# Layer 2's closing: Silu on ScalarE in place of tanh and a product on VectorE

## The chip, the cores and the metric

The kernel runs on one core of one Trainium2 chip. The metric is the device time of one execution in microseconds (us); lower is better. The engines are named as in the profile: PE is TensorE, ACT is ScalarE, DVE is VectorE, POOL is GpSimd.

## The reference, cut to what matters

Four layers follow each other. Each takes x, normalises it, computes a sequence mixer s and a feed-forward result g, and adds their gated product:

```python
xn = _layernorm(x, axis=-1)
s = _L2_attn_ref(xn, ...)                 # windowed attention plus a gated attention on 64 latents, then @ w_out
g = _silu(_L2_ffn_ref(xn, theta, phi, theta_noise, phi_noise))
x = x + s * g

def _L2_ffn_ref(x, theta, phi, theta_noise, phi_noise):
    real = jnp.einsum('bti,io->bto', x, jnp.cos(theta + theta_noise))
    imag = jnp.einsum('bti,io->bto', x, jnp.sin(phi + phi_noise))
    return jnp.sqrt(real * real + imag * imag)
```

x has 8 sequences of 512 tokens with 128 features. The function silu(m) is m / (1 + exp(-m)), which is the same as m (tanh(m/2) + 1) / 2. In layer 2 its argument m is the magnitude, the square root above.

## The kernel before

The whole of x stays in SBUF. Layers 0 to 2 go through it in four chunks of two sequences each (index b is the sequence in its chunk, index c the chunk). Layer 3 then works head by head and takes over half of the time.

Layer 2 is a software pipeline written out by hand. A generator for each engine (`l2_pe`, `l2_dve`, `l2_act`, `l2_pool_engine`) runs over the same slots s = -39 to 37. Each slot holds one unit of windowed and latent attention in several stages: `UNITS2` is 32, eight units in a chunk, each of 128 tokens of one sequence. Work that is done once for a chunk is hung on a slot by `due(d)`, which gives the chunks c with 8c + d = s. So the order of instructions on each engine is fixed by the program, and only semaphores tie the engines to each other. The slots below are counted as in the code; a slot of ACT issues `exponential(s)`, and the same slot of PE ends with `turn_p(s, 0)`, the transposes that need it.

The closing of a chunk goes through these steps:

- `magnitude` (PE) multiplies with the cos and sin matrices; `square` (ACT) squares; `add` (POOL) adds the two squares into the tile moe; `root` (ACT, slot 8c + 3) takes the square root of moe in place.
- `close_tanh(c, b)` (ACT, both at slot 8c + 6) writes tanh(moe / 2) into the tile normed. The one for b = 0 is the first instruction of ACT's slot, ahead of `latent_exponential(s - 1)`. The one for b = 1 stands behind `latent_out(s - 2)` and ahead of `open_copy`, `latent_copy(s - 1)` and `exponential(s)`.
- `close_gate(c, b)` (DVE, slots 8c + 10 and 8c + 11) makes (normed + 1) moe in place. It counts `l2_gated`, on which `close` waits, and on which POOL's `add` of the next chunk waits before it writes moe again.
- `output` (PE, slot 8c + 11) multiplies with w_out; `close` (DVE, slot 8c + 13) multiplies the bank by 0.5 and by normed, and adds the result to x.

The functions that ACT computes in layer 2 are Exp, Tanh, Identity, Square and, once in a chunk, Sqrt. Layer 1 uses Silu, Tanh, Identity and Exp; its first part ends before layer 2's first closing. Layer 3 begins with a Sqrt. Where ACT needs other function tables than those that are active, the compiler puts in an instruction ACT_TABLE_LOAD; the kernel's text does not have it, and the profile books it at the line of the ACTIVATE behind it.

Order of ACT in a slot, the part that matters:

```python
for c in due(6):
    close_tanh(c, 0)
if 0 <= s - 1 < k.UNITS2:
    latent_exponential(s - 1)
...
if 0 <= s - 2 < k.UNITS2:
    latent_out(s - 2)
for c in due(6):
    close_tanh(c, 1)
for c in due(-10):
    open_copy(c, 0)
if 0 <= s - 1 < k.UNITS2:
    latent_copy(s - 1)
...
if 0 <= s < k.UNITS2:
    exponential(s)
```

Of the kernel before, what the change touches and what calls it, by code (L numbers as in the profile page):

```python
# [11 lines left out]
ACT = mybir.ActivationFunctionType  # L12
# [3 lines left out]
D = 128  # L16
# [5 lines left out]
TPB = S // P  # L22
# [23 lines left out]
class Kernel:  # L46
# [1793 lines left out]
    def layer2_prepare(self):  # L1840
        k, io, V, G = self, self.io, self.V, self.G
        W = 32
        k.l2_mom, k.l2_rstd, k.l2_norm, k.l2_pool = (
            Count(k.nc, n) for n in ("l2_mom", "l2_rstd", "l2_norm", "l2_pool"))
        k.l2w_qx, k.l2w_sc, k.l2w_sub, k.l2w_exp = (
            Count(k.nc, n) for n in ("l2w_qx", "l2w_sc", "l2w_sub", "l2w_exp"))
        k.l2w_pTA, k.l2w_pTB, k.l2w_ptA, k.l2w_ptB = (
            Count(k.nc, n) for n in ("l2w_pTA", "l2w_pTB", "l2w_ptA", "l2w_ptB"))
        k.l2w_av, k.l2w_o, k.l2w_oT, k.l2w_go, k.l2g_exp = (
            Count(k.nc, n) for n in ("l2w_av", "l2w_o", "l2w_oT", "l2w_go", "l2g_exp"))  # L1850
        k.l2_add, k.l2_root, k.l2_tanh, k.l2_gated = (
            Count(k.nc, n) for n in ("l2_add", "l2_root", "l2_tanh", "l2_gated"))
        k.l2_filled, k.l2_emptied = k.l1_filled, k.l1_emptied
        k.l2_turn = {}

        flat = k.scratch.rearrange("p i b s -> p (i b s)")
        k.qT2, k.gr2, k.gl2, k.gq2, k.rem2 = ([flat[:, 2048 * i + 1024 * j:2048 * i + 1024 * (j + 1)]
                                               .rearrange("p (b s) -> p b s", b=B) for j in range(2)]
                                              for i in range(5))
        k.oT2 = [flat[:, 10240:11264].rearrange("p (b s) -> p b s", b=B),  # L1860
                 k.hT.rearrange("p (b s) -> p b s", b=B)]
        k.nT2, k.kT2, k.v2_row, k.v2, k.gk2, k.gv2_row, k.gv2 = [], [], [], [], [], [], []
        for j in range(2):
            get = k.part if j else k.own2
            k.nT2.append(get(D, B, W + S + W))
            k.kT2.append(get(D, B, W + S))
            row = get(P, B * 2 * TPB * 288 + 64)
            k.v2_row.append(row)
            k.v2.append(row[:, 0:B * 2 * TPB * 288].rearrange("p (b j w h c) -> p b j w h c", b=B, w=2, h=16, c=9))
            k.gk2.append(get(64, B, 8, 64))  # L1870
            row = get(P, B * 72 + P)
            k.gv2_row.append(row)
            k.gv2.append(row[:, 0:B * 72].rearrange("p (b a h c) -> p b a h c", b=B, a=4, h=2))

        k.pool2 = k.shaped(k.rw_now.rearrange("p i d -> p (i d)")[:, 0:B * 128], (B, 2, 64))
        small = k.rw_before.rearrange("p i d -> p (i d)")
        k.lanes2 = []
        for b in range(B):
            k.lanes2.append(dict(
                mx=small[:, 152 * b:152 * b + 16], gmx=small[:, 152 * b + 16:152 * b + 24],  # L1880
                r=k.shaped(small[:, 152 * b + 24:152 * b + 88], (16, 4)),
                go=k.shaped(small[:, 152 * b + 88:152 * b + 152], (8, 8)),
                qx=k.part(D, 4, 4, W), p=k.part(P, 8, P), pt=k.part(P, 8, P), ox=k.part(P, 4, P),
                sq=k.part(P, 2, 2, D),
                gp=k.sT[:, b * S:(b + 1) * S].rearrange("p (h n) -> p h n", n=64),
                gpt=k.aT[:, b * S:(b + 1) * S].rearrange("p (a n) -> p a n", n=P)))
        k.l2_fills = Count(k.nc, "l2_fills")
# [262 lines left out]
    def l2_dve(self):  # L2150
        k, V, W = self, self.V, 32
# [27 lines left out]
        def divide(w):  # L2179
            c, b, i, t = k.l2_unit(w)  # L2180
            av = k.bank(4, 2).rearrange("p a (n x) -> p (a n) x", x=64)[:, :, 0:36].rearrange("p n (h c) -> p n h c", c=9)
            V.wait_ge(k.l2w_av.sem, w + 1)
            k.step(V.reciprocal(t["r"][:, :, :], av[:, :, :, 8]))
            k.step(V.tensor_tensor(t["r"][:, :, :], t["r"][:, :, :], k.same_head[:, :].unsqueeze(1)
                                   .broadcast_to([P, 16, 4]), ALU.mult))
            k.after(V, k.l2w_oT, w - 1)
            V.tensor_tensor(t["ox"].rearrange("p j (g h d) -> p (j g) h d", h=4, d=8), av[:, :, :, 0:8],
                            t["r"][:, :, :].unsqueeze(3).broadcast_to([P, 16, 4, 8]),
                            ALU.mult).then_inc(*k.l2w_o.up())
# [11 lines left out]
        def latent_largest(w):  # L2201
            c, b, i, t = k.l2_unit(w)
            k.l2_filled_by(V, b, "latent_scores", w)
            k.step(V.tensor_reduce(t["gmx"][:, :], k.bank(6 + b).rearrange("p (h n) -> p h n", n=64), AX.X, ALU.max))

        def latent_subtract(w):
            c, b, i, t = k.l2_unit(w)
            if w < 2:
                k.after(V, k.gated, 2 * CHUNKS)
            V.tensor_tensor(t["gp"], k.bank(6 + b).rearrange("p (h n) -> p h n", n=64),  # L2210
                            t["gmx"][:, :].unsqueeze(2).broadcast_to([P, 8, 64]),
                            ALU.subtract).then_inc(*k.l2_emptied[b].up())
# [52 lines left out]
            k.l2_emptied_of(V, b, "gate_remote", c, b)  # L2265
            k.stt(gr, gr, 1.0, k.bank(6 + b), ALU.add, ALU.mult).then_inc(*k.l2_emptied[b].up())

        def close_gate(c, b):
            tiles = slice(b * TPB, (b + 1) * TPB)
            t = k.normed[:, tiles, :]  # L2270
            V.wait_ge(k.l2_tanh.sem, 2 * c + b + 1)
            k.stt(t, t, 1.0, k.moe[:, tiles, :], ALU.add, ALU.mult).then_inc(*k.l2_gated.up())

        def close(c, b):
            t = k.normed[:, b * TPB:(b + 1) * TPB, :]
            x = k.xs[:, c * NT + b * TPB:c * NT + (b + 1) * TPB, :]
            V.wait_ge(k.l2_gated.sem, 2 * c + b + 1)
            k.l2_filled_by(V, b, "output", c, b)
            k.step(k.stt(t, k.bank(6 + b).rearrange("p (t d) -> p t d", d=D), 0.5, t, ALU.mult, ALU.mult))
            V.tensor_tensor(x, x, t, ALU.add).then_inc(*k.l2_emptied[b].up())  # L2280

        for s, due in k.l2_slots():
            if 0 <= s - 3 < k.UNITS2:
                divide(s - 3)
            if 0 <= s - 2 < k.UNITS2:
                latent_largest(s - 2)
            if 0 <= s - 3 < k.UNITS2:
                gate_o(s - 3)
            if 0 <= s - 2 < k.UNITS2:
                latent_subtract(s - 2)  # L2290
            for c in due(12):
                mix(c, 0)
                mix(c, 1)
            for c in due(13):
                close(c, 0)
                close(c, 1)
            if 0 <= s + 1 < k.UNITS2:
                queries_spread(s + 1)
            for c in due(10):
                close_gate(c, 0)  # L2300
            for c in due(-14):
                open_scale(c, 1)
            for c in due(-21):
                open_moments(c, 1)
            for c in due(-3):
                pool(c, 0)
            for c in due(-2):
                latents(c, 0)
                latents(c, 1)
            if 0 <= s - 1 < k.UNITS2:  # L2310
                largest(s - 1)
            for c in due(11):
                close_gate(c, 1)
            for c in due(-3):
                pool(c, 1)
            if 0 <= s - 1 < k.UNITS2:
                subtract(s - 1)
            for c in due(-15):
                open_scale(c, 0)
            for c in due(-22):  # L2320
                open_moments(c, 0)
            if 0 <= s - 3 < k.UNITS2:
                latent_divide(s - 3)
            yield

    def l2_act(self):
        k, A, W = self, self.A, 32
# [80 lines left out]
            A.wait_ge(k.l2_add.sem, 4 * c + 4)  # L2408
            A.activation(k.moe[:, :, :], k.moe[:, :, :], ACT.Sqrt).then_inc(*k.l2_root.up())

        def close_tanh(c, b):
            tiles = slice(b * TPB, (b + 1) * TPB)
            A.wait_ge(k.l2_root.sem, c + 1)
            if c:
                k.l2_emptied_of(A, b, "output", c - 1, b)
            else:
                k.after(A, k.l1_closed, 2 * CHUNKS)
            A.activation(k.normed[:, tiles, :], k.moe[:, tiles, :], ACT.Tanh, scale=0.5).then_inc(*k.l2_tanh.up())

        for s, due in k.l2_slots():  # L2420
            for c in due(-6):
# [2 lines left out]
            for c in due(-4):  # L2424
                values(c, 1, 0)
            for c in due(6):
                close_tanh(c, 0)
            if 0 <= s - 1 < k.UNITS2:
                latent_exponential(s - 1)
            for c in due(3):  # L2430
# [6 lines left out]
            if 0 <= s - 2 < k.UNITS2:  # L2437
                latent_out(s - 2)
            for c in due(6):
                close_tanh(c, 1)  # L2440
            for c in due(-10):
                open_copy(c, 0)
            if 0 <= s - 1 < k.UNITS2:
# [1136 lines left out]
```

## Time and profile before

| what | value |
| --- | --- |
| median of 3 runs | 3213.32 us (3204.18 to 3224.15) |
| the profiled execution | 3207.89 us, its span 3205.2 us |
| granted clock of PE, mean | 0.976 |
| PE busy | 3074.6 us, 96% of the span |
| DVE busy | 2382.3 us, 74% |
| ACT busy | 1830.3 us, 57%, 4246 instructions |
| POOL busy | 856.6 us, 27% |

The span runs from the first to the last instruction; 2.7 us lie around it. Layer 2's units run from about 1060 to 1500 us of the span. Busy time is what an engine spent in its instructions; waits count as idle. The granted clock is PE's clock as a share of its full speed.

### The profile page before, as it was taken

The page shows a single profiled execution, that of the slowest core. Times are in us where ns is not written, and L with a number is a line of the kernel's source. Part 1 is how long each engine was busy: PE and PEld are TensorE (multiplying, and loading weights), DVE is VectorE, ACT ScalarE, POOL GpSimd, SP SyncE. Part 2 cuts the span into 40 slices and gives each one's busy share as a digit, 9 for nine tenths or more (in the row PEclk, how much of TensorE's full clock was granted, in tenths as well). Part 3 has the DMA queues.
Part 4 walks back from the last instruction along what each step waited for, and adds up shares of the span by engine and source line. Part 5 has one row for each costly group of instructions (what it writes and reads, how often), then busy time and mean ns, then how long its engine had stood idle before and what let it go on. Part 6 is the DMA issues. An engine that isn't in the chain of part 4 may idle for free. (4 is left out here: it accounts for less than half of the span.)

```text
span 3205.2 us, 57936 instructions
## 1 busy us (share of the span) xinstructions
PE 3074.6 (96%) x20342; PEld 2414.1 (75%) x20342; DVE 2382.3 (74%) x5012; ACT 1830.3 (57%) x4246; POOL 856.6 (27%) x707
## 2 busy tenths in 40 slices
PE   5999998999999999997899999999999999999998
PEld 4777775566665677775778888888888888888887
DVE  4777876556556555556867888888888888888888
ACT  2445554545655444442756666666666666666666
POOL 2101101101101100001523444444344443444443
PEclk9999998999999899998999999999999999999999
DMA  2000101000000000002001000111000111000000
GB/s 55 2 4 28 53 27 50 1 1 1 1 1 1 1 1 1 1 1 68 14 1 23 20 12 15 22 22 23 12 20 14 23 22 23 9 22 15 23 1 27
DMA packets 43555, 53.08 MB, mean 17 GB/s; under 512 B 8646, under 2 KB 27273, under 8 KB 43273
## 3 DMA queue, kind: packets, MB, share of 16 engines
q1 hardware_dynamic: 39298, 47.02, 5.9%
q8 instruction: 168, 2.75, 0.4%
q10 hardware_dynamic: 3974, 2.37, 0.3%
q14 instruction: 115, 0.93, 0.1%
HBM read 38.63 MB, written 10.75 MB: 15 GB/s over the span
## 5 line engine op out<-in xcount | busy, mean ns | idle before, releaser
L75 PE MATMUL banks<-scratch 128*128 128x128 f32 (+3 forms) x3648 | 715.5, 325 | 11.5 <-ACT scratch L2974 8.9
L75 PEld LDWEIGHTS banks<-scratch 128*128 128x128 f32 x3648 | 482.8, 192 | 77.0 <-issue 60.0
L75 PE MATMUL banks<-lower 128*128 128x128 f32 (+2 forms) x2688 | 508.8, 355 | 4.3 <-DVE lower L1453 3.7
L75 PEld LDWEIGHTS banks<-lower 128*128 128x128 f32 (+1 forms) x2688 | 343.7, 193 | 170.4 <-issue 169.4
L75 PEld LDWEIGHTS banks<-scratch,tb 128*128 128x128 f32 x2560 | 356.6, 191 | 101.9 <-issue 61.5
L75 PE MATMUL banks<-scratch,tb 128*128 128x128 f32 x2560 | 368.5, 275 | 0.0
L3417 POOL TENSOR_TENSOR scratch<-scratch,aT 128x1024 f32<-128x1024 f32 x128 | 358.8, 2803 | 4.5 <-DVE aT L3239 4.5
L83 DVE SCALAR_TENSOR_TENSOR scratch<-scratch,tb 128x512 f32<-128x512 f32 (+3 forms) x512 | 340.0, 705 | 8.4
L3409 POOL TENSOR_TENSOR scratch<-backwards,nn 128x512 f32<-128x512 f32 x128 | 133.3, 1042 | 736.1 <-ACT nn L3329 736.1
L83 DVE SCALAR_TENSOR_TENSOR scratch<-tb,nn,banks 128x512 f32<-128x512 f32 (+3 forms) x512 | 267.8, 544 | 75.6 <-PE banks L75 71.5
L3239 DVE TENSOR_TENSOR aT<-banks,turn 64x1024 f32<-64x1024 f32 x256 | 312.9, 1222 | 5.7
L3352 ACT ACTIVATE scratch<-banks 128x384 f32<-128x384 f32 (+1 forms) x384 | 200.0, 521 | 183.0 <-PE banks L79 183.0
L75 PE MATMUL banks<-nT,w 128*128 128x512 f32 x544 | 283.0, 604 | 2.6 <-PEq L69 1.4
L3343 ACT ACTIVATE scratch<-scratch,mn 128x512 f32<-128x512 f32 (+3 forms) x512 | 282.7, 566 | 0.4 <-DVE mn L3273 0.2
L3229 DVE TENSOR_TENSOR scratch<-banks,turn 128x512 f32<-128x512 f32 x256 | 176.5, 689 | 138.3 <-PE banks L75 137.1
L3273 DVE CUSTOM_DVE_ANT_0 scratch<-scratch,tb,coef 128x512 f32<-128x512 f32 (+3 forms) x512 | 261.8, 549 | 0.0
L75 PEld LDWEIGHTS banks<-minus_half,sT 128*128 128x128 f32 x2048 | 239.6, 192 | 2.0 <-ACT sT L3322 2.0
L75 PE MATMUL banks<-minus_half,sT 128*128 128x1 f32 x2048 | 236.8, 245 | 1.2 <-ACT sT L3318 1.2
L1453 DVE TENSOR_TENSOR lower<-lower,banks 128x512 f32<-128x512 f32 x160 | 108.7, 685 | 161.1 <-ACT lower L1662 161.1
L79 PEld LDWEIGHTS banks<-ident,scratch 128*128 128x128 f32 x1408 | 171.0, 141 | 72.4 <-issue 69.6
L79 PE MATMUL banks<-ident,scratch 128*128 128x128 f32 x1408 | 219.2, 273 | 2.4 <-ACT scratch L3343 1.4
L3335 ACT ACTIVATE scratch<-scratch 128x384 f32<-128x384 f32 (+1 forms) x384 | 215.3, 561 | 8.1 <-DVE scratch L83 6.4
(421 smaller groups left out, 4954.8 us busy)
## 6 DMA issues: line engine op xcount, KB each, us to landing
tb<-head_rows SPq DMA_DIRECT2D x32, 512.0 KB, 7.1
turn<-head_turns SPq DMA_DIRECT2D x64, 128.0 KB, 2.7
head_turns<-loads SPq DMA_DIRECT2D x16, 256.0 KB, 2.8
head_turns<-rotation SPq DMA_DIRECT2D x16, 256.0 KB, 3.1
xs<-in_x SPq DMA_DIRECT2D x8, 256.0 KB
w<-in_L_Wqk SPq DMA_DIRECT2D x16, 128.0 KB, 2.1
out<-xs SPq DMA_DIRECT2D x8, 256.0 KB, 2.3
lower<-in_L_w1T SPq DMA_DIRECT2D x1, 1280.0 KB, 9.2
```

The source lines that it names most:

```text
L75: return self.T.matmul(out, lhsT, rhs, start=start, stop=stop, skip_group_check=True)
L79: return self.T.matmul(out, in_, self.ident[0:n, 0:n], start=start, stop=True, is_transpose=True, skip_group_check=True)
L83: return self.V.scalar_tensor_tensor(out, a, s, b, op0, op1)
L1453: V.tensor_tensor(k.hidden[:, e % 2, m, b * S:(b + 1) * S], k.gated_h[:, m, :], k.bank(2 * m + 1), ALU.mult).then_inc(*k.l1_hid[m].up())
L3229: V.tensor_tensor(t["qk"][:, i * S:(i + 1) * S], k.bank(2 + i), hd["turn"][:, 0, :], ALU.mult).then_inc(*(k.h_ck if i else k.h_cq).up())
L3239: x = V.tensor_tensor(k.sines[there, :].rearrange("p (i s) -> p i s", i=2), k.bank(2, 2)[here, :, :], hd["turn"][here, 1, :].unsqueeze(1). ...
L3273: x = V.tensor_tensor_reduce(y, y, view(hd["tb"][:, 2, i * P + 127:i * P + 128], [[-1, n]]), k.coef[:, h:h + 1], 3e38, ALU.add, ALU.min, t ...
L3335: A.activation(y, y, ACT.Ln, bias=1.0).then_inc(*k.h_ln.up())
L3343: x = A.activation(y, y, ACT.Exp, bias=t["mn"][:, i:i + 1], scale=-1.0, accum_out=t["sum"][:, i:i + 1])
L3352: A.activation(t["pt"][:, lo:hi], k.bank(7 if piece == 1 else 6)[:, 0:hi - lo], ACT.Identity).then_inc(*k.h_pt.up())
L3409: G.tensor_tensor(t["dk"][:, :, :], k.backwards[:, :].unsqueeze(1).broadcast_to([P, 4, P]), t["nn"][:, 4:8].unsqueeze(2).broadcast_to([P, ...
L3417: G.tensor_tensor(t["qk"], t["qk"], k.sines, ALU.add).then_inc(*k.h_rot.up())
```

## The change

The ACT step writes silu(moe) instead of tanh(moe / 2), and the DVE product disappears. The last DVE step no longer multiplies by 0.5. The semaphore `l2_gated` is now counted by ACT at slot 8c + 6, no longer by DVE at slots 8c + 10 and 8c + 11.

```diff
-        def close_gate(c, b):                      # DVE
-            tiles = slice(b * TPB, (b + 1) * TPB)
-            t = k.normed[:, tiles, :]
-            V.wait_ge(k.l2_tanh.sem, 2 * c + b + 1)
-            k.stt(t, t, 1.0, k.moe[:, tiles, :], ALU.add, ALU.mult).then_inc(*k.l2_gated.up())
-
         def close(c, b):                           # DVE
-            V.wait_ge(k.l2_gated.sem, 2 * c + b + 1)
+            k.after(V, k.l2_gated, 2 * c + b + 1)
             k.l2_filled_by(V, b, "output", c, b)
-            k.step(k.stt(t, k.bank(6 + b).rearrange("p (t d) -> p t d", d=D), 0.5, t, ALU.mult, ALU.mult))
+            k.step(V.tensor_tensor(t, k.bank(6 + b).rearrange("p (t d) -> p t d", d=D), t, ALU.mult))
             V.tensor_tensor(x, x, t, ALU.add).then_inc(*k.l2_emptied[b].up())
...
-            for c in due(10):                      # DVE's slots, ahead of open_scale, pool, latents, largest
-                close_gate(c, 0)
...
-            for c in due(11):                      # DVE's slots, between largest and subtract
-                close_gate(c, 1)
...
-        def close_tanh(c, b):                      # ACT
+        def close_gate(c, b):
             tiles = slice(b * TPB, (b + 1) * TPB)
             A.wait_ge(k.l2_root.sem, c + 1)
             if c:
                 k.l2_emptied_of(A, b, "output", c - 1, b)
             else:
                 k.after(A, k.l1_closed, 2 * CHUNKS)
-            A.activation(k.normed[:, tiles, :], k.moe[:, tiles, :], ACT.Tanh, scale=0.5).then_inc(*k.l2_tanh.up())
+            A.activation(k.normed[:, tiles, :], k.moe[:, tiles, :], ACT.Silu).then_inc(
+                *k.l2_gated.up())
...
             for c in due(6):
-                close_tanh(c, 0)
+                close_gate(c, 0)
...
             for c in due(6):
-                close_tanh(c, 1)
+                close_gate(c, 1)
```

The helper `after` waits for the same count, and leaves the wait out only where the count is not positive.

## Rows read from the trace of the kernel before

**Rows 1.** The page's chain that ended last: shares of the span by engine.
```profile
PE 48%; DVE 1%; ACT 0%; issue 0%; ACTq 0%; DVEq 0%
```

**Rows 2.** Windows: layer 2, busy us (instructions) of PE, PEld, DVE, ACT, POOL; clock, DMA.
```profile
1060.00:1500.00 440.00, 425.70 (x3041) 333.22 (x3039) 249.43 (x467) 181.37 (x300) 23.35 (x33) 0.94 0.01 2
```

**Rows 3.** Who PE waited for, 1060 to 1500 us: us in total, times, longest.
```profile
PE banks L79 <- ACT lower L2332: 1.3, 2, 0.7
PE banks L75 <- DVE lower L2187: 1.1, 1, 1.1
...
PE banks L79 <- DVE rw_before L2219: 0.6, 1, 0.6
```

**Rows 4.** Groups of ACT by line: count | busy us, mean ns | idle before.
```profile
L1662 ACT ACT_TABLE_LOAD x21 | 26.9, 1283 | 0.4
...
L1710 ACT ACT_TABLE_LOAD x4 | 5.1, 1283 | 0.1
...
L2418 ACT ACTIVATE normed<-moe 128x512 f32<-128x512 f32 x8 | 5.0, 628 | 0.0
...
L1728 ACT ACTIVATE normed<-moe 128x512 f32<-128x512 f32 x4 | 2.5, 622 | 0.0
```

**Rows 5.** Timeline of ACT in layer 1: start, duration, what.
```profile
700.98 1.28 ACT L1662 ACT_TABLE_LOAD   x1
703.60 0.60 ACT L1662 ACTIVATE lower<-banks 128x512 f32<-128x512 f32 x1 [1.34 <-PE banks L75]
```

**Rows 6.** Timeline of ACT, layer 2, slot 3.
```profile
1116.58 0.60 ACT L2349 ACTIVATE aT<-banks 128x512 f32<-128x512 f32 x1 [0.17 <-PE banks L79]
1117.19 1.28 ACT L2332 ACT_TABLE_LOAD   x1
1118.49 1.06 ACT L2332 ACTIVATE lower<-lower 128x1024 f32<-128x1024 f32 x1
```

**Rows 7.** Timeline of PE, layer 2, slot 3.
```profile
1119.60 0.66 PE L79 MATMUL banks<-ident,lower 128*128 128x128 f32 x4 [0.68 <-ACT lower L2332]
```

**Rows 8.** Timeline of ACT, layer 2, slot 6.
```profile
1156.18 0.27 ACT L2355 ACTIVATE scratch<-banks 64x128 f32<-64x128 f32 x1 [5.13 <-PE banks L79]
1156.35 0.62 ACT L2418 ACTIVATE normed<-moe 128x512 f32<-128x512 f32 x1
1157.26 0.60 ACT L2360 ACTIVATE upper<-banks 128x512 f32<-128x512 f32 x1 [0.28 <-PE banks L79]
1157.75 0.59 ACT L2349 ACTIVATE aT<-banks 128x512 f32<-128x512 f32 x1
1158.23 1.06 ACT L2332 ACTIVATE lower<-lower 128x1024 f32<-128x1024 f32 x1
```

**Rows 9.** Timeline of PE, layer 2, slot 6.
```profile
1157.06 0.60 PE L79 MATMUL banks<-ident,sT 128*128 128x128 f32 x4
1157.91 0.39 PE L75 MATMUL banks<-maskg,identb 128*128 128x512 bf16 x1 [0.25 <-ACT upper L2360]
...
1160.20 0.63 PE L79 MATMUL banks<-ident,lower 128*128 128x128 f32 x4
```

**Rows 10.** Timeline of ACT, layer 2, slot 22.
```profile
1382.00 0.62 ACT L2418 ACTIVATE normed<-moe 128x512 f32<-128x512 f32 x1
1382.52 0.58 ACT L2349 ACTIVATE aT<-banks 128x512 f32<-128x512 f32 x1
1382.99 1.05 ACT L2332 ACTIVATE lower<-lower 128x1024 f32<-128x1024 f32 x1
```

**Rows 11.** Timeline of PE, layer 2, slot 22.
```profile
1384.44 1.32 PE L79 MATMUL banks<-ident,lower 128*128 128x128 f32 x8
```

**Rows 12.** Windows of 4 us around slots 21 and 22, columns as in rows 2.
```profile
1364.00:1368.00 4.00, 3.24 (x30) 3.05 (x28) 0.86 (x3) 3.33 (x6) 0.00 (x0) 1.00 0.00 0
...
1376.00:1380.00 4.00, 4.00 (x32) 3.93 (x30) 0.43 (x2) 0.70 (x2) 0.00 (x0) 0.71 0.00 0
1380.00:1384.00 4.00, 4.00 (x23) 2.85 (x22) 1.84 (x4) 2.18 (x4) 0.00 (x0) 0.86 0.00 0
```

**Rows 13.** Windows of 4 us at layer 2's beginning, columns as in rows 2.
```profile
1072.00:1076.00 4.00, 3.37 (x8) 1.57 (x8) 1.62 (x3) 2.85 (x3) 0.00 (x0) 0.50 0.00 0
```

**Rows 14.** Timeline of DVE, slot 10: the product that the change removes.
```profile
1185.57 0.69 DVE L83 SCALAR_TENSOR_TENSOR normed<-normed,moe 128x512 f32<-128x512 f32 x1
1186.17 1.55 DVE L89 TENSOR_SCALAR n<-xs,mv,rstd 128x128 f32<-128x128 f32 x4
```

More of the change, by code:

```diff
@@ L1850, in layer2_prepare @@
             Count(k.nc, n) for n in ("l2w_av", "l2w_o", "l2w_oT", "l2w_go", "l2g_exp"))
-        k.l2_add, k.l2_root, k.l2_tanh, k.l2_gated = (
-            Count(k.nc, n) for n in ("l2_add", "l2_root", "l2_tanh", "l2_gated"))
+        k.l2_add, k.l2_root, k.l2_gated = (
+            Count(k.nc, n) for n in ("l2_add", "l2_root", "l2_gated"))
         k.l2_filled, k.l2_emptied = k.l1_filled, k.l1_emptied
```

## The prediction

> **What bounds the kernel now.** I read the chain that ended last first. Of the span, 48% of it lies on PE, and the other engines hold 1% or nothing [rows 1]. The reader should see that only work that makes PE wait can cost time. Next I read the stage that the change touches. In the 440 us of layer 2, PE is busy 425.70 us, DVE 249.43 and ACT 181.37, at a clock of 0.94 [rows 2]. ACT has more than half of its time free, so what matters is not how much ACT gains but where in its order. Third I read who PE waited for in this stage: the longest waits are around 1 us, and the exponential of line 2332 is among them with two waits, 1.3 us together [rows 3]. PE's order in layer 2 is so tight that a step of ACT or DVE that comes 1 us later shows up. Nothing catches it up afterwards, since nearly all of DVE's and ACT's later work waits for PE.
>
> **What the change adds: table loads.** Layer 1 has Silu and Exp on the same engine. Its exponentials stand at five lines, each of which ran 4 times and has 4 ACT_TABLE_LOADs of 1283 ns (one line stands for the five), and the Silu of line 1662 has 21 loads [rows 4]. So Silu and Exp share no set of tables, and each change between them costs a load. In layer 2, each chunk now issues in slot 8c + 6: Silu, `latent_exponential` (Exp), `latent_out` (Identity), Silu, `open_copy` and `latent_copy` (Identity), `exponential` (Exp). Identity runs under any set, as slot 3 shows: after the Sqrt, the Identity of line 2349 runs, and the load stands right before the Exp [rows 6]. This gives four loads a chunk, 16 in all, and 16 x 1.283 = 20.5 us of ACT. Before, these Tanhs had none.
>
> One load costs a little over its own time: from the start of the Identity to the start of the Exp it is 1118.49 - 1116.58 = 1.91 us with a load between them, against 1158.23 - 1157.75 = 0.48 without one [rows 6, 8]. That is 1.43 us. A load does not wait for the semaphore of its ACTIVATE: in layer 1 it ran at 700.98 while the ACTIVATE behind it stood until 703.60 [rows 5]. So a load hides wherever ACT would be idle anyway.
>
> A rule of the Trainium skill speaks against this change. "ScalarE: Activation LUTs", section "Table sets: the hidden batching unit", says to batch activations by set and not by function, and the change mixes two sets four times a chunk where it had one.
>
> **First pair of loads, at the head of the slot.** They push `latent_exponential` by 2 x 1.43 = 2.86 us. Behind it ACT sits idle for 5.13 us, and PE's transposes of its result start at 1157.06, 6 us after its end at 1156.18 - 5.13 = 1151.05 [rows 8, 9]. The idle time hides them: cost 0. If that cover were gone, up to 2.86 us a chunk would appear, 11.4 in all.
>
> **Second pair, in the middle of the slot.** Here the queue behind the Silu is dense: `open_copy`, `latent_copy`, `exponential`, and PE waits for two of them.
>
> Slot 6 (chunk 0): the Silu starts at 1156.35 + 1.43 = 1157.78 instead of 1156.35. `open_copy` was released at 1157.26 and can now start about 0.5 later than the Silu, at 1158.27, which is 1.0 us late. PE's latent scores wait for just this copy (0.25 us now) [rows 9], so PE is 1.0 late here. The second load comes before `exponential`: its start moves by 1.0 + 1.43 = 2.43 us. It ended at 1158.23 + 1.06 = 1159.29, and PE's transposes `turn_p` started at 1160.20 [rows 8, 9], so 0.91 us are free. PE began 0.05 us after the exponential in the place where it did wait (1119.60 against 1119.55) [rows 6, 7]. PE becomes late by 2.43 - 0.91 + 0.05 = 1.57 us. This takes in the 1.0 us before. Chunk 1 repeats the pattern with the same gaps.
>
> Slot 22 (chunk 2): there is no later chunk to open, so no `open_copy` and no idle gap that soaks up part of it. The exponential moves by the full 2.86 us. It ended at 1382.99 + 1.05 = 1384.04, and PE started at 1384.44 [rows 10, 11]: free are 0.40. PE becomes late by 2.86 - 0.40 + 0.05 = 2.51 us. Chunk 3 repeats it.
>
> The sum is 2 x 1.57 + 2 x 2.51 = 8.2 us. Slot 3 of the kernel before is a witness: one load, right before an exponential, and PE waited 0.68 us [rows 7].
>
> **What it may add through the clock.** After the stretch 1364 to 1368, in which PE was busy for 3.24 of 4 us at full clock, the granted clock fell to 0.71 and 0.86 in two windows of 4 us [rows 12]. This means a share of the time at 1.2 GHz in place of 2.4 GHz. It lost 0.29 x 4 + 0.14 x 4 = 1.7 us of work at full speed. The same follows PE's idle time in chunks 0 and 1. The four new stalls are larger than the idle time in that window (0.76 us). No row shows what a stall of this length does in this place, so the bounds are 0 and 4 x 1.7 = 6.8 us. I take two falls, 3.4 us, for the two longer stalls of chunks 2 and 3, because those are nearest to that row or above it, while chunks 0 and 1 have falls of their own shortly after.
>
> **What it removes.** Eight products on DVE of 0.69 us, of which 1186.17 - 1185.57 = 0.60 us is time that the next one could use [rows 14]: at most 4.8 us. They stand in slots 10 and 11 ahead of the largest or the subtraction of the next unit. PE's waits for DVE in the whole stage are 1.1 us and 0.6 us once each (a third, at the seam to layer 1, has nothing to do with the gate) and belong to the last units, not to these slots [rows 3]. I take 0. PE is what DVE waits for; DVE only idles 0.6 us more. In the drain of the pipeline the product of chunk 3 stands before one of those waits; its gain is between 0 and 0.6, and I take 0 since DVE had also to wait for the values from PE.
>
> **What changes at equal cost.** Silu on a 128x512 tile took 622 ns, the Tanh 628 [rows 4]: 0. The last product without the 0.5 remains one pass of a PSUM bank and an SBUF tile: 0. POOL's `add` for the next chunk may start four slots earlier, as `l2_gated` comes earlier. ACT's `square` and `root` behind it never waited for POOL, so nothing moves: 0. No DMA is issued or passed.
>
> **Sum.** 8.2 + 3.4 = 11.6 us. On the profiled execution this gives a span of 3216.8 and a time of 3219.5 us. That execution lies 5.4 us under the median of the runs, so against the median it is 3213.3 + 11.6 = 3224.9 us.
>
> **The rivals.** (1) Faster: the loads find cover and DVE's relief counts. The mechanism is DVE's order in slots 10 and 11: with 0.60 us less ahead of the largest and the subtraction, the next exponential and `turn_p` come earlier. It gives 8 x 0.60 = 4.8 us less, 3208.5 us. It decides from the point where PE waits for the subtraction in these slots and the exponential has over 2.9 us of room in slot 8c + 6. For it speaks that ACT is idle for half of the stage; against it, that the room is 0.91 and 0.40 us, and that PE waits for no DVE step in slots 10 and 11. Chance 0.07.
>
> (2) The switch costs more than the load: ACT's queue is emptied before each. As a mechanism of this kernel, priced at once more the load's own 1.28 us for each of the two switches on the path in a chunk, it adds 4 x 2 x 1.28 = 10.3 us: 3235 us. Against it: 1116.58 + 0.60 = 1117.18, and the load starts at 1117.19, the Exp 0.02 us after its end [rows 6]; there is no room for an emptying of this size. Chance 0.04. The Trainium skill, "ScalarE: Activation LUTs", section "What ACT_TABLE_LOAD costs", states 1283 ns for the load plus a drain of about 1380 ns for every switch, by which this rival would be right, at some 3236 us. With the load this trace agrees to the ns, and the drain does not appear in it.
>
> (3) The clock reacts strongly. At layer 2's beginning it stayed at 0.50 in the window 1072 to 1076 and the next [rows 13]. Eight such us cost 4 us of work. After each of the four stalls that is 16 us in place of 3.4: 3213.3 + 8.2 + 16 = 3237.5 us. For it: the new stalls are the longest of the stage. Against it: that stretch came at the end of layer 1, where PE had stood longer. Chance 0.1.
>
> (4) The change adds no loads, because a set with both functions is chosen. Then 3213 us. Layer 1 speaks against it in all 20 of its exponentials [rows 4]. Chance 0.03.
>
> (5) The forecast: loads in the middle of the slot on PE's path, with none to four falls of the clock, 8 to 15 us: 3221 to 3228. Chance 0.76.
>
> **How the numbers follow.** The predicted time is the forecast's, 3225. The runs before lie within 9 us below and 11 us above their median, more than the effect, so the range needs some 8 us on either side for that; with case 1 it begins at 3207, with case 3 it ends at 3240. Within 1%, 32 us, is about what a measurement of this kernel can tell from no change. All cases lie inside it, and only case 3 with an unlucky set of runs reaches beyond: faster 0.01, same 0.96, slower 0.03.
>
> **What the profile after would show.** 16 more ACT_TABLE_LOADs, eight at the Silu's line and eight at the two exponentials' lines, ACT busy 20 us longer, DVE busy 5.5 us less. PE waits for the exponential in slots 6, 14, 22 and 30 by 0.6 to 2.5 us on top of a wait for `open_copy` of 1.2 in the first two; layer 2 ends 8 to 15 us later, and layers 0, 1 and 3 have their length of before. The prediction is wrong if the loads are fewer, if PE passes through those slots without a wait, or if the granted clock in them moves by more than in one window each.

## The result, and the profile after

The changed kernel took 3224.48 us (median of 20 runs, 3207.09 to 3236.73), the kernel before in the same comparison 3212.83 us (20 runs, 3198.79 to 3225.98). The ratio is 1.0040 with an interval of 1.0024 to 1.0056: the change costs 12.8 us (7.7 to 18.0), small but clear of the noise. The forecast was 3225 us and 11.6 us more.

The profiled execution took 3220.08 us, its span is 3218.8 us. Its ACT is busy for 1850.9 us in 4262 instructions, 20.6 us and 16 instructions more than before; DVE for 2376.8 us, 5.5 us less; PE's mean clock is 0.975 (0.976).

Who PE waited for in layer 2, 1060 to 1510 us (engine, line waited for: us in total, times, longest), to hold against [rows 3]. Lines behind the removed step are up to 10 lower: L2322 is the exponential (L2332), L2350 the open copy (L2360), L2345 `latent_out` (L2355), L2334 `latent_exponential` (L2344).

```profile
PE banks L79 <- ACT lower L2322: 6.8, 6, 2.3
PE banks L75 <- ACT lower L2350: 2.1, 2, 1.3
...
PE banks L75 <- ACT upper L2350: 1.3, 1, 1.3
PE banks L75 <- DVE lower L2187: 1.1, 1, 1.1
```

The exponential went from 2 waits and 1.3 us to 6 waits and 6.8 us; the waits for DVE are those of before, but for one of 0.2 us. Of the 2.1 us for the lower open copy, 0.83 us are no cost of the change: the kernel before has this wait too, at 1059.4 us, just ahead of its window. The groups of ACT by line show where the loads stand, with L2408 as the Silu (busy, mean ns, idle before):

```profile
L2322 ACT ACT_TABLE_LOAD x9 | 11.5, 1283 | 0.2
L2408 ACT ACT_TABLE_LOAD x8 | 10.3, 1283 | 0.1
...
L2334 ACT ACT_TABLE_LOAD x4 | 5.1, 1283 | 0.1
L2408 ACT ACTIVATE normed<-moe 128x512 f32<-128x512 f32 x8 | 5.0, 630 | 0.1
```

That is 8 + 4 + 4 = 16 more (the exponential had 5), and the Silu itself takes as long as the Tanh did [rows 4]. ACT's timeline of slot 6, to hold against [rows 8]:

```profile
1150.37 1.28 ACT L2408 ACT_TABLE_LOAD   x1
1151.67 0.63 ACT L2408 ACTIVATE normed<-moe 128x512 f32<-128x512 f32 x1
1152.32 1.28 ACT L2334 ACT_TABLE_LOAD   x1
1153.61 0.63 ACT L2334 ACTIVATE sT<-sT 128x512 f32<-128x512 f32 x1
1156.51 0.27 ACT L2345 ACTIVATE scratch<-banks 64x128 f32<-64x128 f32 x1 [2.27 <-PE banks L79]
1156.80 1.28 ACT L2408 ACT_TABLE_LOAD   x1
1158.10 0.63 ACT L2408 ACTIVATE normed<-moe 128x512 f32<-128x512 f32 x1
1158.63 0.58 ACT L2350 ACTIVATE upper<-banks 128x512 f32<-128x512 f32 x1
1159.11 0.59 ACT L2339 ACTIVATE aT<-banks 128x512 f32<-128x512 f32 x1
1159.71 1.28 ACT L2322 ACT_TABLE_LOAD   x1
1161.01 1.06 ACT L2322 ACTIVATE lower<-lower 128x1024 f32<-128x1024 f32 x1
```

The first two loads ran in ACT's idle time, which shrank from 5.13 to 2.27 us. The other two stand in a row of work without a gap. PE in slot 6, against [rows 9], and below it in slot 22, against [rows 11]:

```profile
1159.26 0.39 PE L75 MATMUL banks<-maskg,identb 128*128 128x512 bf16 x1 [1.27 <-ACT upper L2350]
...
1162.12 0.66 PE L79 MATMUL banks<-ident,lower 128*128 128x128 f32 x4 [0.40 <-ACT lower L2322]
...
1390.49 1.09 PE L79 MATMUL banks<-ident,lower 128*128 128x128 f32 x8 [2.34 <-ACT lower L2322]
```

The waits of slot 14 repeat those of slot 6 and that of slot 30 repeats that of slot 22, to 0.01 us. The new idle time of PE is 2 x (1.27 - 0.25 + 0.40) + 2 x 2.34 = 7.5 us. The profile counts idle time from the modelled end of the product ahead, and in the kernel before `turn_p` started up to 0.16 us ahead of that end (1383.52 + 1.08 = 1384.60 against 1384.44 in slot 22). So the start times are the better measure of what a stall costs. Against the kernel before, and less the lag that PE already had in that slot, `turn_p` starts 1.59 us later in slots 6 and 14, 2.50 in slot 22 and 2.51 in slot 30: 8.2 us in all. The rest of the difference is clock. Windows of 4 us behind slot 22 (busy us and instructions of PE, PEld, DVE, ACT, POOL; clock; DMA), to hold against [rows 12]:

```profile
1387.00:1391.00 4.00, 1.66 (x14) 1.48 (x14) 3.41 (x6) 3.41 (x4) 0.72 (x1) 1.00 0.00 0
1391.00:1395.00 4.00, 4.00 (x28) 3.30 (x26) 1.12 (x1) 1.60 (x3) 0.00 (x0) 0.58 0.00 0
1395.00:1399.00 4.00, 4.00 (x24) 3.88 (x23) 0.00 (x0) 0.00 (x0) 0.00 (x0) 0.50 0.02 4
1399.00:1403.00 4.00, 4.00 (x23) 3.67 (x22) 1.09 (x4) 0.42 (x2) 0.00 (x0) 0.64 0.00 0
```

Right behind the stall, PE is busy without a gap but at half clock for most of 12 us: 0.42 x 4 + 0.50 x 4 + 0.36 x 4 = 5.1 us are below full clock. In the kernel before, this stretch ran at full clock:

```profile
1387.00:1391.00 4.00, 4.00 (x44) 3.93 (x43) 1.98 (x4) 0.00 (x0) 0.00 (x0) 1.00 0.02 4
1391.00:1395.00 4.00, 4.00 (x27) 2.75 (x25) 2.40 (x6) 1.81 (x3) 0.00 (x0) 1.00 0.00 0
1395.00:1399.00 4.00, 3.94 (x41) 3.33 (x40) 3.61 (x5) 1.71 (x3) 0.00 (x0) 1.00 0.00 0
```

The same wait of 2.34 us in slot 30 was followed by one such window only:

```profile
1483.00:1487.00 4.00, 1.66 (x11) 1.13 (x10) 3.22 (x6) 3.75 (x5) 0.00 (x0) 1.00 0.00 0
1487.00:1491.00 4.00, 4.00 (x23) 4.00 (x23) 1.30 (x3) 1.71 (x3) 0.00 (x0) 0.57 0.01 2
1491.00:1495.00 4.00, 4.00 (x28) 2.85 (x27) 2.17 (x4) 1.81 (x3) 0.00 (x0) 1.00 0.00 0
```

That is 0.43 x 4 = 1.7 us. So the length of the wait alone does not say what the clock takes.

The start of the exponential shows both, the stalls and the clock, in steps against the kernel before: 0.33 us later in unit 5, 6.39 in unit 22, 10.51 in unit 23, 14.26 in unit 31. Behind layer 2 nothing more is added; the span as a whole is 13.6 us longer. So this execution holds 8.2 us of stalls and 13.6 - 8.2 = 5.4 us of clock. Windows of 5 us, from the first exponential of layer 2 to 25 us behind its last, agree: 30.8 us below full clock against 25.7 in the kernel before.

### The profile page after: what moved, and what is told of

It is laid out like the page before. It is cut to its first block and busy times, and to the rows that moved or that the text cites. A ratio compares the mean times of both kernels' runs of the same rounds, so it can differ in the third digit from the quotient of the medians.

```text
span 3218.8 us, 57941 instructions
## 1 busy us (share of the span) xinstructions
PE 3079.3 (96%) x20342; PEld 2420.0 (75%) x20342; DVE 2376.8 (74%) x5004; ACT 1850.9 (58%) x4262; POOL 856.0 (27%) x707
```

## The experiments

"Above" is the ratio less 1, times the median of the kernel before on the same chip. The two last columns split the mean span: PE's mean granted clock times the span, and the rest, the part below full clock. This is a book-keeping of the records, with a standard error of 1 to 3 us; a wait that falls into low clock is counted in the first part by half. The first row has no split against the kernel before, since no clocks of that kernel are recorded beside it.

| kernel | runs | above before, us (95%) | span x clock, less that of before | below full clock, us (before) |
| --- | --- | --- | --- | --- |
| the change | 20 | 12.8 (7.7 to 18.0) | | 87.4 |
| Silus at the head | 12 | 0.3 (-6 to 7) | 0.8 | 76.7 (79.6) |
| delay by Identity | 7 | 20.5 (12 to 29) | 7.9 | 90.3 (79.6) |
| product kept | 12 | 11.2 (4.5 to 17.6) | 8.0 | 82.3 (79.6) |
| product gone | 12 | -1.9 (-9 to 5) | 0.1 | 76.4 (79.6) |
| stall filled | 12 | 13.8 (8 to 19) | 6.3 | 88.4 (80.1) |
| one load in the middle | 12 | 1.0 (-4 to 5) | 3.9 | 77.6 (80.1) |
| longer stall | 4 | 37.9 (30 to 47) | 13.8 | 104.7 (80.1) |
| the change again | 12 | 16.4 (10 to 23) | 8.2 | 89.0 (80.1) |
| long stall filled | 7 | 22.5 (14 to 30) | 20.4 | 79.8 (76.7) |
| long stall again | 4 | 38.5 (30 to 47) | 13.5 | 103.0 (76.7) |

**Silus at the head.** Both Silus at the start of the slot, no other edit.

```diff
             for c in due(6):
                 close_gate(c, 0)
+                close_gate(c, 1)
             if 0 <= s - 1 < k.UNITS2:
                 latent_exponential(s - 1)
...
-            for c in due(6):
-                close_gate(c, 1)
             for c in due(-10):
                 open_copy(c, 0)
```

> Both Silus stand together at the head of slot 8c + 6, so a chunk has two table loads more than the kernel before in place of four, and none of them stands between the latent copy and the exponential. Theory (only loads in the middle of the slot cost time, since ACT sits idle for over 4 us behind the head of the slot): PE has no new wait in slots 6, 14, 22 and 30, layer 2 ends within 2 us of where it ends in the kernel before, time within 3 us of it. Rival (each load costs its time wherever it stands, or ACT's load as such matters): half of the change's cost stays, 5 to 7 us.

Measured: 3204.39 against 3208.05 us, ratio 1.0001 (0.9981 to 1.0021). ACT in slot 6:

```profile
1139.33 1.28 ACT L2408 ACT_TABLE_LOAD   x1
1140.63 1.15 ACT L2408 ACTIVATE normed<-moe 128x512 f32<-128x512 f32 x2
1141.80 1.28 ACT L2334 ACT_TABLE_LOAD   x1
1143.09 0.63 ACT L2334 ACTIVATE sT<-sT 128x512 f32<-128x512 f32 x1
...
1145.42 0.59 ACT L2339 ACTIVATE aT<-banks 128x512 f32<-128x512 f32 x1
1145.90 1.06 ACT L2322 ACTIVATE lower<-lower 128x1024 f32<-128x1024 f32 x1
```

No load stands before the exponential, 0.48 us lie between its start and that of the copy ahead of it, and PE's waits for it are 1.3 us in all, as in the kernel before. Two of the four loads are gone, the other two are free. The cost of the change is one of places, not of Silu.

**Delay by Identity.** The kernel before, with two idle activations where the change has its second pair of loads.

```diff
...
+        def delay():
+            k.after(A, k.l2_delay, k.l2_delay.n)
+            A.activation(k.delay2[:, :, :], k.ones[:, :].unsqueeze(1).broadcast_to([P, 13, P]),
+                         ACT.Identity).then_inc(*k.l2_delay.up())
...
             for c in due(6):
+                delay()
                 close_tanh(c, 1)
...
+            for c in due(6):
+                delay()
             if 0 <= s < k.UNITS2:
                 exponential(s)
```

> The kernel before, with tanh and the DVE product, and two extra Identity activations of 128x1664 in slot 8c + 6: one ahead of the second tanh and one ahead of the exponential, where the changed kernel has its table loads. No table load is added; their output is used by nothing. Theory (a load in this place is nothing but a delay of the exponential): PE waits at the same four places, about 1.3 and 0.4 us in slots 6 and 14 and 2.3 us in slots 22 and 30, and layer 2 ends some 8 to 14 us later, time 8 to 15 us above the kernel before. Rival (table loads cost by something of their own, such as an emptying of the queue or a slower first activation): clearly less than the changed kernel, under 5 us.

Measured: ratio 1.0064 (1.0037 to 1.0091). Without an added table load, span times clock grew by 7.9 us, close to the 8.2 of the changed kernel. PE waited 7.1 us for the exponential (6.8) and 1.3 us each in two slots for the open copy. The time is higher than I gave, 20.5 us against 8 to 15, but its interval overlaps with that of the change. A load in this place is a delay of its length, and nothing beyond it shows.

**Product kept.** The changed kernel, with DVE's step back in its old slots, as a maximum of the tile with itself.

```diff
...
+        def kept(c, b):
+            t = k.normed[:, b * TPB:(b + 1) * TPB, :]
+            V.wait_ge(k.l2_silu.sem, 2 * c + b + 1)
+            k.stt(t, t, 1.0, t, ALU.mult, ALU.max).then_inc(*k.l2_gated.up())
...
+            for c in due(10):
+                kept(c, 0)
...
+            for c in due(11):
+                kept(c, 1)
...
             A.activation(k.normed[:, tiles, :], k.moe[:, tiles, :], ACT.Silu).then_inc(
-                *k.l2_gated.up())
+                *k.l2_silu.up())
```

> The changed kernel, with the DVE product put back in its old place as an operation that leaves its operand as it is (maximum of normed with itself), and POOL again released by it. Theory (the DVE work taken away was under cover): within 2 us of the changed kernel, 10 to 14 us above the kernel before. Rival (DVE's relief gave something back and hid a part of the loads' cost): 3 to 5 us slower than the changed kernel.

Measured: ratio 1.0035 (1.0014 to 1.0055), and 8.0 us by span times clock. By time alone the 3 to 5 us of the rival would still fit into the interval; by span times clock, 8.0 us beside the 8.2 of the changed kernel, putting DVE's work back costs nothing that shows.

**Product gone.** The kernel before without the DVE product, which leaves that part of the gate out.

```diff
-            for c in due(10):
-                close_gate(c, 0)
...
-            for c in due(11):
-                close_gate(c, 1)
...
-            ... ACT.Tanh, scale=0.5).then_inc(*k.l2_tanh.up())
+            ... ACT.Tanh, scale=0.5).then_inc(*k.l2_gated.up())
```

> The kernel before, with the tanh, but without the DVE product (that part of the computation is left out), and the semaphore of the gate counted by ACT as in the changed kernel. No table load is added. Theory: no gain, within 1.5 us of the kernel before in layer 2. Rival (DVE in slots 10 and 11 is on the path): 2 to 5 us faster.

Measured: ratio 0.9994 (0.9973 to 1.0015), and 0.1 us by span times clock. The interval alone would allow a gain of the 2 to 5 us of the rival, but PE's list of waits is the one of before and the book-keeping shows nothing. Both ways round, the DVE work was under cover, that is, done while PE had other work.

**Stall filled.** The changed kernel; PE does idle products while it waits in slots 22 and 30.

```diff
         def turn_p(w, half):
-            T.wait_ge(k.l2w_exp.sem, w + 1)
             k.after(T, k.l2w_go if half else k.l2w_o, w)
+            if w in (22, 30) and not half:
+                for n in (384, 384, 256):
+                    k.mm(k.bank(4)[:, 0:n], k.ident[:, :], k.wqkv2.rearrange("p i d -> p (i d)")[:, 0:n])
+            T.wait_ge(k.l2w_exp.sem, w + 1)
```

> The changed kernel, and in slots 22 and 30 PE issues three products that nothing uses (384, 384 and 256 columns, some 2.1 us) into the bank of the transposes while it would wait for the exponential. The wait itself stays, only PE is busy in it. Theory (part of the change's cost is the granted clock falling after a stall of 2.3 us: in three profiles with that stall, the step from exponential 22 to 23 was 4.1 us longer than in the kernel before): this step comes back to within 0.2 us of the kernel before, 30 to 31 too, and the time lies 3 to 5 us under the changed kernel, 8 to 9 us above the kernel before. Rival (the falls come at times of their own and only chance put one there): the step stays long or the low clock appears in another slot, and the time is that of the changed kernel.

Measured: ratio 1.0043 (1.0026 to 1.0060), 88.4 us below full clock. The step from exponential 22 to 23 went from 13.96 us to 10.91 (9.84 before), so the fall right behind the stall was mostly gone in the profiled execution, though not wholly. In the mean over runs nothing was gained: the low clock is that of the changed kernel. My expectation for the time missed. This experiment alone would speak for the rival. Two things stand beside that reading. The profiled execution is the fastest of the twelve (3214.13 us against a median of 3225.54), so its profile isn't typical of the mean. And in it the units behind the filled slots 22 and 30 lost 1.7 and 0.0 us to low clock, those behind the unfilled slots 6 and 14 lost 3.4 and 3.5.

**One load in the middle.** The second Silu right behind the latent exponential.

```diff
             if 0 <= s - 1 < k.UNITS2:
                 latent_exponential(s - 1)
+            for c in due(6):
+                close_gate(c, 1)
...
-            for c in due(6):
-                close_gate(c, 1)
             for c in due(-10):
                 open_copy(c, 0)
```

> The changed kernel with the second Silu moved up to stand right behind the latent exponential. Three of the four loads of a chunk are then in the idle time of ACT, and one alone, that of the exponential, stands in the middle. From the rows of before: exponential 1.43 us later by the load and, in slots 22 and 30, 0.49 earlier since the gate has left this place; free are 0.91 (slots 6, 14) and 0.40 us (22, 30). Theory: PE waits 0.5 to 0.6 us for the exponential in each of the four slots and not for the open copy beyond the 0.25 us of before, 2 to 3 us in all, no fall of the clock after 22, time 1 to 5 us above the kernel before. Rival (loads cost wherever they are): as the changed kernel, 11 us and more.

Measured: ratio 1.0003 (0.9988 to 1.0017), 3.9 us by span times clock. ACT and PE in slot 22:

```profile
1387.04 0.63 ACT L2408 ACTIVATE normed<-moe 128x512 f32<-128x512 f32 x1
1387.58 0.25 ACT L2345 ACTIVATE scratch<-banks 64x128 f32<-64x128 f32 x1
```

```profile
1387.89 0.39 PE L75 MATMUL banks<-maskg,identb 128*128 128x512 bf16 x1 [1.11 <-ACT scratch L2345]
...
1390.73 1.09 PE L79 MATMUL banks<-ident,lower 128*128 128x128 f32 x8 [0.40 <-ACT lower L2322]
```

The wait for the exponential fell from 2.34 to 0.40 us. In slot 22 the unit behind it still lost 1.7 us to low clock, where I had expected no fall. The three loads at the head no longer fit into ACT's idle time where the slots are short, and `latent_out` came 1.11 us late for PE, which I had not worked out. Two loads in the middle are clearly set apart all the same: there the ratios are 1.0040 and 1.0051, with one in the middle 1.0003, with none 1.0001. One and none are not told apart by time, only by span times clock (3.9 against 0.8 us).

**Longer stall.** The changed kernel with two of the idle activations ahead of the exponential (the same `delay()` as above, called twice).

> The changed kernel with two more Identity activations of 128x1664 (1.47 us each, used by nothing) ahead of the exponential in slot 8c + 6. Theory (once the slack is used up, each us of ACT in this place is a us of PE's): PE's waits for the exponential grow by 2.9 us in each of the four slots, 11.8 us in all, and the time lies 12 us above the changed kernel or more, 24 to 30 us above the kernel before, the excess being low clock. Rival (later slots take up part of a delay): under 8 us above the changed kernel.

Measured: ratio 1.0118 (1.0092 to 1.0145). PE's waits for the exponential rose by 17.4 - 6.8 = 10.6 us, nearly the 11.8 of the delays, and the time by over 20 us. No later slot takes up anything. The time came out above the 24 to 30 us that I gave: 104.7 us lay below full clock, 25 more than in the kernel before.

**The change again.** The changed kernel beside these three.

> The changed kernel once more, beside the other three on the same chip. 8 to 16 us above the kernel before. Its profile shows the same waits at the same four places; where the clock falls tells which falls repeat: after slot 22 by every theory of mine, elsewhere differently.

Measured: ratio 1.0051 (1.0030 to 1.0072). The waits are 2.34 us in slots 22 and 30 again, and the step from 22 to 23 is 13.97 us, as in the first profile of the change (13.96), the Identity kernel (13.96) and the kernel with the product kept (13.96). Slot 6 differs from what I expected: PE waited 1.27 us for the open copy, the products behind it ran at half clock (0.57 and 0.58 in the next two windows of 4 us), and PE came too late to wait for the exponential.

**Long stall filled, and unfilled again.** The longer stall, with PE doing idle products in all four slots.

```diff
         def turn_p(w, half):
...
+            k.after(T, k.l2w_go if half else k.l2w_o, w)
+            if w % 8 == 6 and not half:
+                for n in (384, 384, 384, 384) + ((384, 384, 128) if w > 16 else ()):
+                    k.mm(k.bank(4)[:, 0:n], k.ident[:, :], k.wqkv2.rearrange("p i d -> p (i d)")[:, 0:n])
             T.wait_ge(k.l2w_exp.sem, w + 1)
-            k.after(T, k.l2w_go if half else k.l2w_o, w)
```

> The kernel with the longer stall (the changed kernel and two Identity activations of 128x1664 ahead of the exponential), and PE issues products that nothing uses while it would wait there: 4 x 384 columns (3.2 us) in slots 6 and 14, 6 x 384 + 128 (5.0 us) in slots 22 and 30. The delays stay as they are. Theory (what the longer stall costs beyond its length is low clock that follows idle time of PE): beyond the length of the delays, some 19 us, little is left: 18 to 26 us above the kernel before, its share of span below full clock back near 80 us (the kernel before's), 10 to 20 us under the unfilled one. Rival (the low clock has nothing to do with PE's idling): time and clock as the unfilled one, 38 us above the kernel before.

> The kernel with the longer stall once more, unfilled, beside the filled one on the same chip: 29 to 46 us above the kernel before by its first interval, some 105 us of the span below full clock.

Measured on the same chip: filled 3230.68 us, ratio 1.0070 (1.0045 to 1.0094), unfilled 3248.20 us, 1.0120 (1.0093 to 1.0146). Below full clock lay 79.8 against 103.0 us, with 76.7 in the kernel before. PE behind the stall of slot 22, unfilled and then filled:

```profile
1409.23 1.97 PE L79 MATMUL banks<-ident,lower 128*128 128x128 f32 x8 [5.44 <-ACT lower L2324]
1410.99 1.06 PE L75 MATMUL banks<-mask_first,identb 128*128 128x512 bf16 x2
```

```profile
1391.68 4.34 PE L75 MATMUL banks<-wqkv,ident 128*128 128x384 f32 x14
1397.29 1.09 PE L79 MATMUL banks<-ident,lower 128*128 128x128 f32 x8 [1.27 <-ACT lower L2327]
1398.22 0.59 PE L75 MATMUL banks<-mask_first,identb 128*128 128x512 bf16 x2
```

The same two bf16 products take 1.06 us behind the idle stall and 0.59 behind the filled one. ACT's delays are the same in both kernels; PE's waits for the exponential are 17.4 us unfilled and 4.6 us filled. So the 17.5 us between them come from the low clock that follows PE's idle time. By span times clock the filled kernel is 20.4 us above the kernel before; the length of the delays by the sum of the prediction is 8.2 + 4 x 2.94 = 20.0.

## Why the prediction was right

- **The loads, their number and place**: 16 more, eight at the Silu and eight at the two exponentials, as forecast. In the second pair, the load of the exponential stood behind the Identities, right before its Exp.
- **The first pair is free**: shown by the profile (idle time left: 2.27 us) and by the kernel with both Silus at the head.
- **The second pair, 8.2 us**: right, and to a few hundredths of a us. By start times the profile has 1.59 us in slots 6 and 14 (1.57 forecast), 2.50 and 2.51 in slots 22 and 30 (2.51 forecast), 8.2 in all; span times clock says 8.2 for the change measured again. The idle times that the profile prints, 7.5 us in all, are the smaller figure for the reason given above.
- **The clock, 3.4 us**: the mis-sized term. The change has 87 to 89 us below full clock against 80, some 8 more, and the two other kernels with the same waits have 3 and 11 more. That is at or above the prediction's upper bound of 6.8 us, as far as an error of 1 to 3 us lets one say. The mechanism was right, and the long stall shows it, but the size came from a row with 0.76 us of idle time and a loss of 1.7 us. Behind 2.34 us of idle time the profile has 5.1 us below full clock in slot 22 and 1.7 us in slot 30. One of the prediction's own signs of being wrong came true here: behind slot 22 the clock fell in three windows of 4 us, not in one.
- **The total**: 11.6 us against 12.8 and 16.4, both with intervals that hold it. That it came so near to the first is in part luck: 8.2 and some 8 us of clock make 16, and the interval of 7.7 to 18.0 us is wide enough to hide the 5 us that the clock's term lacked.
- **DVE's relief, 0**: the product put back and the product taken out alone both say so.
- **Rival 1** (faster) fell with these two. **Rival 2** (an emptied queue at each switch) fell with the Identity delays, which cost no less than the loads, and with the timeline, in which a load starts 0.02 us after the activation before it. **Rival 3** (a strong reaction of the clock, 16 us) overstated the size, though the direction was right: some 8 us in the change lie between the 3.4 of the forecast and its 16, and with stalls about twice as long it was 25. **Rival 4** (no loads) fell with the count.

What stays open: how much of the low clock of the change comes right behind its own stalls. The four profiles with these stalls (the change twice, the Identity delays, the product kept) narrow it down. From one exponential's start to the next, each of them lost 5.2 us to low clock behind slot 22 and 1.7 us behind slot 30, where the kernel before lost nothing in either place. Behind slot 6 it was 0.0, 4.5, 3.4 and 4.5 us. So the stalls of the first two chunks can cost as much clock as the longer ones, and in some executions nothing. Filling slots 22 and 30 took most of the fall there out of the profile but not out of the mean. The waits of slots 6 and 14 for the open copy, 1.27 us each, were filled in no kernel, since the bank that PE waits for there is the one at issue.

## What to carry to other kernels

Ask of an activation not what it takes but which set of tables is active before and behind it: one Silu between exponentials is two loads of 1.28 us, and they come on top of ACT's order at that point, whatever share of the time ACT is idle. Then lay the loads into the idle time: two Silus side by side at the head of the slot made the same change free. A DVE step saved is worth what the list of waits says, here nothing, in a kernel where DVE waits for PE.

## What the runs showed of the hardware that I had not expected

- An idle PE costs more than its idle time. With 17.4 us of waits for the exponential, 103 to 105 us of the span lay below full clock against 77 to 80. With the same delays and PE kept busy by products that nothing uses (4.6 us of waits left), it was 79.8 us, and the kernel was 17.5 us faster.
- After an idle stretch of 5.4 us, PE went on at half clock at once; after 2.34 us in slot 22, the 4 us with the stall still showed 1.00 and the next 4 us 0.58. How long the low clock lasts is not settled by the length of the stall: after the same 2.34 us it was three windows of 4 us in slot 22 and one in slot 30.
- The fall behind a wait of 2.3 to 2.5 us in slot 22 repeated to 0.01 us in four executions of three kernels (13.96 to 13.97 us from exponential 22 to 23). Elsewhere in layer 2 the falls come at places that differ from one execution to the next, in steps of some 1.6 us. They go with the spread between executions of one kernel: the slower ones have the lower mean clock.
